# Second expert stage of a fused block: where the last chunk's routing stands, the order of two steps, and the work of the last two steps

## The reference

```python
logits = xt @ router_w.T
topk_vals, topk_idx = jax.lax.top_k(logits, TOP_K)      # 2 of 8
g = jax.nn.sigmoid(topk_vals)
g = g / (g.sum(axis=-1, keepdims=True) + 1e-10)
for e in range(E):
    ge = jnp.sum(jnp.where(topk_idx == e, g, jnp.zeros_like(g)), axis=-1)
    h = jax.nn.silu(xt @ w_gate[e]) * (xt @ w_up[e])
    out = out + ge[:, None] * (h @ w_down[e])
```

## Time and profile before

| | us |
|---|---|
| median of 3 runs | 830.08 |
| lowest, highest | 828.88, 831.36 |
| the profiled execution | 829.33 |
| its span in the trace | 827.4 |
| PE busy in it | 780.4 (94%) |
| VectorE | 625.3 (76%) |
| ScalarE | 526.0 (64%) |
| POOL | 425.5 (51%) |

### The profile page before, as it was taken

How to read it: one execution, slowest core, us unless ns; L and a number is a source line. 1 busy time by engine, 2 the same in 40 slices (tenths; PEclk the granted TensorE clock), 3 DMA queues, 4 the chain that set the end, 5 groups by cost and what they waited for, 6 DMA issues and landing times.

```text
span 827.4 us, 13529 instructions
## 1 busy us (share of the span) xinstructions
PE 780.4 (94%) x4328; PEld 546.0 (66%) x4328; DVE 625.3 (76%) x1596; ACT 526.0 (64%) x1162; POOL 425.5 (51%) x446
## 2 busy tenths in 40 slices
PE   4989899998799999999999999999999998699996
PEld 2667688886556666666666656666666676588884
DVE  7998678788898766778667597667787677587785
ACT  5566566656667767767757577667667545466653
POOL 1054999974344334424334333343335345499974
PEclk9999999999999999999999999999999999899998
DMA  8012663390000000000000000000011332243201
GB/s 229 1 42 29 136 123 77 66 361 2 2 1 1 1 2 1 1 1 1 1 1 2 1 2 1 1 2 1 10 31 32 39 78 67 52 81 101 65 17 39
DMA packets 51141, 35.16 MB, mean 42 GB/s; under 512 B 2640, under 2 KB 48592, under 8 KB 51072
## 3 DMA queue, kind: packets, MB, share of 16 engines
q1 hardware_dynamic: 51072, 34.30, 16.8%
HBM read 33.04 MB, written 1.25 MB: 41 GB/s over the span
## 4 chain that ended last, share of the span: by engine, by line
PE 66%; DVE 12%; POOL 10%; issue 7%; ACT 4%; DMA 1%; SPq 0%; POOLq 0%; DVEq 0%; ACTq 0%
PE psum L935 14%; PE psum L917 12%; PE psum L902 11%; POOL hid_lo L749 9%; PE psum L249 7%; PE psum L250 5%; PE psum L251 5%; PE psum L520 5%; PE psum L859 4%; DVE prob L1030 2%; ACT x_norm L315 1%; DVE hid L638 1%; DVE hid L618 1%; DVE ln_stats L264 1%; DMA ssm_par<-in_ssm_par 1%
## 5 line engine op out<-in xcount | busy, mean ns | idle before, releaser
L1291 POOL TENSOR_SCALAR prob<-prob,ones 128x512 f32<-128x512 f32 x256 | 175.0, 697 | 271.1 <-DVE ones L1019 271.1
L1198 ACT ACTIVATE prob<-prob,ones 128x512 f32<-128x512 f32 x256 | 183.6, 719 | 124.4 <-DVE ones L1030 124.4
L749 POOL TENSOR_TENSOR hid_lo<-hid,hid_hi 128x512 fp32r<-128x512 f32 x128 | 192.2, 1518 | 82.3 <-ACT hid_hi L567 81.3
L1030 DVE CUSTOM_DVE_ANT_0 prob<-psum,bias_band 128x512 f32<-128x512 f32 x256 | 161.6, 687 | 71.4 <-PE psum L902 70.9
L618 DVE TENSOR_TENSOR hid<-silu,psum 128x512 f32<-128x512 f32 x128 | 87.1, 684 | 54.0 <-PE psum L251 43.6
L638 DVE TENSOR_TENSOR hid<-hid,gate_all 128x512 f32<-128x512 f32 x118 | 115.1, 977 | 14.6 <-DMA gate_all<-gates 1.8
L935 PE MATMUL psum<-probT,v 128*64 128x512 f32 x512 | 124.0, 605 | 0.0
L560 ACT ACTIVATE silu<-psum 128x512 f32<-128x512 f32 x128 | 76.4, 598 | 74.6 <-PE psum L251 73.6
L917 PE MATMUL psum<-ident,prob 128*128 128x128 f32 x1024 | 123.3, 273 | 0.0
L917 PEld LDWEIGHTS psum<-ident,prob 128*128 128x128 f32 x1024 | 114.6, 140 | 10.3 <-issue 2.9
L567 ACT CAST hid_hi<-hid 128x512 fp32r<-128x512 f32 x128 | 78.5, 618 | 48.7 <-DVE hid L638 45.2
(11 more groups left out here) (154 smaller groups left out, 1205.9 us busy)
## 6 DMA issues: line engine op xcount, KB each, us to landing
gate_all<-gates SPq DMA_DIRECT2D x59, 256.0 KB, 5.3
bias_band<-bias_rows SPq DMA_DIRECT2D x16, 448.0 KB, 9.0
w_raw<-in_w_gate SPq DMA_DIRECT2D x16, 128.0 KB, 2.8
w_raw<-in_w_up SPq DMA_DIRECT2D x16, 128.0 KB, 2.8
w_raw<-in_w_down SPq DMA_DIRECT2D x16, 128.0 KB, 3.7
x_res<-in_x SPq DMA_DIRECT2D x4, 256.0 KB, 5.8
out<-x_res SPq DMA_DIRECT2D x4, 256.0 KB, 2.3
wqT<-in_WqT SPq DMA_DIRECT2D x1, 512.0 KB, 7.7
```

The source lines that it names most:

```text
L749: nc.gpsimd.tensor_tensor(m["hid_lo"][:, s % 2, half, :], m["hid"][:, s % DEEP, half, :], m["hid_hi"][:, s % 2, half, :].bitcast(F32), ALU ...
L1030: nc.vector.tensor_tensor_reduce(out=prob[:, buf, h, :], in0=bank[scores_home(n) + h][:, :], in1=row_bias, scale=-1.0, scalar=NEG_START, o ...
L1198: nc.scalar.activation(prob[:, buf, h, :], prob[:, buf, h, :], ACT.Exp, bias=peak[:, buf, h:h + 1], scale=-1.0, accum_out=total[:, buf, h: ...
L1291: nc.gpsimd.tensor_scalar(prob[:, buf, h, :], prob[:, buf, h, :], inv[:, buf, h:h + 1], 1.0, ALU.mult, ALU.mult).then_inc(a_n, 1)
```

## The change

It does two things, both in the second expert stage (k = 1).

**Routing of the last chunk.** On PE, step 6 is opened: `gate_up(6,0)` and `down(4)` now stand ahead of `route_logits`; step 8 is issued in `leave` too, and `route_turn` stands between its `down(6)` and `gate_up(8,1)`, `route_spread` behind that. On VectorE `route_weights` moves ahead of step 7's first product, and `route_pick` ahead of its second. On ScalarE `gates_copy` moves behind step 8's first silu and `high_of(7,1)`. The generic loops begin at step 9 for PE and ScalarE. In `LAST_CHUNK_LATE` the steps 9 and 10 are exchanged: (2,2) is now step 9 and (1,3) step 10.

**The end.** The low parts of (step 30, half 1), (31,0) and (31,1) go from POOL to VectorE (`last_low`, semaphore `hd`). The copy of chunk 2's sums goes ahead of step 31's second silu. `last_down` takes the six matmuls in the order hi·hi, lo·hi, hi·lo for each half and waits for each part only where it is used. The copy, the turn, the add and the output of chunk 3 are done in two halves of 256 columns (`last_sums`, `last_turn`, `last_add`).

The diff:

```diff
--- before.py
+++ after.py
@@ -218,7 +218,7 @@
 
         def moe_sems(k):
             names = ("lg", "lc", "rt", "ex", "ld0", "ld1", "sp", "wu", "wd", "g", "u", "sg", "mul", "gm", "hi", "hl", "d",
-                     "acc", "gt_in", "gt_t", "gt_c", "gd", "gb", "y", "yt")
+                     "acc", "gt_in", "gt_t", "gt_c", "gd", "gb", "y", "yt", "hd", "ya")
             q = {n: sem(f"moe{k}_{n}") for n in names}
             q["bc"] = [[sem(f"moe{k}_bc{par}{c}") for c in range(CH)] for par in range(2)]
             return q
@@ -344,7 +344,7 @@
         LAG = 2
         STEPS_K = CH * E
         BY_CHUNK = [(0, 0), (0, 1), (1, 0), (1, 1), (0, 2), (0, 3), (1, 2), (1, 3)]
-        LAST_CHUNK_LATE = [(0, 0), (0, 1), (1, 0), (1, 1), (0, 2), (1, 2), (2, 0), (2, 1), (0, 3), (1, 3), (2, 2), (2, 3),
+        LAST_CHUNK_LATE = [(0, 0), (0, 1), (1, 0), (1, 1), (0, 2), (1, 2), (2, 0), (2, 1), (0, 3), (2, 2), (1, 3), (2, 3),
                            (3, 0), (3, 1), (3, 2), (3, 3)]
         PAIRWISE = [(0, 0), (1, 0), (0, 1), (1, 1), (0, 2), (1, 2), (0, 3), (1, 3)]
         BY_EXPERT = [(0, 0), (0, 1), (0, 2), (0, 3), (1, 0), (1, 1), (1, 2), (1, 3)]
@@ -510,7 +510,11 @@
 
             q, m, (e, c) = MOE[k], MEM[k], ORDER[k][s]
             w_hi, w_lo = weights_of(k, e)
-            pe.wait_ge(q["hl"], 2 * s + 2)
+            if k == 1 and s == STEPS_K - 2:
+                pe.wait_ge(q["hl"], 2 * s + 1)
+                pe.wait_ge(q["hd"], 1)
+            else:
+                pe.wait_ge(q["hl"], 2 * s + 2)
             if s == FIRST[k][e]:
                 pe.wait_ge(q["wd"], e + 1)
             for h in range(MT):
@@ -537,7 +541,7 @@
 
         def experts_tensor(pe, k, turn_in):
 
-            for s in range(8, END + 4):
+            for s in range(8 + k, END + 4):
                 expert_step(pe, k, s)
             expert_step(pe, k, END + 4)
             sums_turn(pe, k, 0)
@@ -550,6 +554,33 @@
             gate_up(pe, k, END + 7, 1)
             down(pe, k, END + 6)
 
+        def last_down(pe):
+
+            q, m, s = MOE[1], MEM[1], STEPS_K - 1
+            e, c = ORDER[1][s]
+            w_hi, w_lo = weights_of(1, e)
+            assert (e, c) == (E - 1, CH - 1)
+            for h in range(MT):
+                col = slice(2 * FH + h * D, 2 * FH + (h + 1) * D)
+                hh, hl = m["hid_hi"][:, s % 2, h, :], m["hid_lo"][:, s % 2, h, :]
+                for n, (w, r) in enumerate(((w_hi, hh), (w_lo, hh), (w_hi, hl))):
+                    if n == 0:
+                        pe.wait_ge(q["hi"], 2 * s + h + 1)
+                    if n == 2:
+                        pe.wait_ge(q["hd"], h + 2)
+                    last = nc.tensor.matmul(bank[4 + c][:, :], w[:, col], r, start=False,
+                                            stop=(h == MT - 1 and n == 2), skip_group_check=True)
+            last.then_inc(q["d"], 1)
+
+        def last_turn(pe):
+            c = CH - 1
+            for part in range(2):
+                pe.wait_ge(MOE[1]["ya"], part + 1)
+                for n in (2 * part, 2 * part + 1):
+                    last = nc.tensor.transpose(bank[part][:, (n % 2) * P:(n % 2 + 1) * P],
+                                               MEM[1]["y_sum"][:, c, n * P:(n + 1) * P], ident[:, :])
+                last.then_inc(MOE[1]["yt"], 1)
+
 
 
         def silu_of(act, k, s, half):
@@ -604,8 +635,17 @@
             high_of(act, k, END + 6, 1)
             if k == 0:
                 ln_high(act, 2, 0, 4)
+            else:
+                sums(act, k, 2)
             silu_of(act, k, END + 7, 1)
             high_of(act, k, END + 7, 0)
+
+        def last_sums(act):
+            c = CH - 1
+            act.wait_ge(MOE[1]["d"], STEPS_K)
+            for part in range(2):
+                cols_ = slice(2 * P * part, 2 * P * (part + 1))
+                nc.scalar.copy(MEM[1]["y_sum"][:, c, cols_], bank[4 + c][:, cols_]).then_inc(MOE[1]["ya"], 1)
 
 
 
@@ -675,14 +715,41 @@
                 gated(dve, 0, END + 6, 1)
             else:
                 vector_step(dve, k, END + 5)
-                vector_step(dve, k, END + 6)
+                product(dve, 1, END + 6, 0)
+                gated(dve, 1, END + 6, 0)
+                product(dve, 1, END + 6, 1)
+                gated(dve, 1, END + 6, 1)
+                product(dve, 1, END + 7, 0)
+                gated(dve, 1, END + 7, 0)
+                last_low(dve, END + 6, 1)
+                product(dve, 1, END + 7, 1)
+                gated(dve, 1, END + 7, 1)
+                last_low(dve, END + 7, 0)
+                add_sums(dve, 1, 1)
+                last_low(dve, END + 7, 1)
+                add_sums(dve, 1, 2)
+                for part in range(2):
+                    last_add(dve, part)
+                return
             add_sums(dve, k, 1)
             product(dve, k, END + 7, 0)
             gated(dve, k, END + 7, 0)
-            if k == 0:
-                ln_low(dve, 2, 0, 4)
+            ln_low(dve, 2, 0, 4)
             product(dve, k, END + 7, 1)
             gated(dve, k, END + 7, 1)
+
+        def last_low(dve, s, half):
+            q, m = MOE[1], MEM[1]
+            dve.wait_ge(q["hi"], 2 * s + half + 1)
+            dve.wait_ge(q["d"], s - 1)
+            nc.vector.tensor_tensor(m["hid_lo"][:, s % 2, half, :], m["hid"][:, s % DEEP, half, :],
+                                    m["hid_hi"][:, s % 2, half, :].bitcast(F32), ALU.subtract).then_inc(q["hd"], 1)
+
+        def last_add(dve, part):
+            dve.wait_ge(MOE[1]["yt"], CH + part)
+            n = (CH - 1) * QT + 2 * part
+            xc = x[:, n:n + 2, :].rearrange("p n d -> p (n d)")
+            nc.vector.tensor_tensor(xc, bank[part][:, 0:2 * P], xc, ALU.add).then_inc(MOE[1]["acc"], 1)
 
 
 
@@ -1004,10 +1073,15 @@
                 part(4, 1)
                 ln_turn(pe, 3, 3, JOB_BANK)
                 expert_step(pe, 1, 5)
+                gate_up(pe, 1, 6, 0)
+                down(pe, 1, 4)
                 route_logits(pe, 1, 3, JOB_BANK)
-                expert_step(pe, 1, 6)
+                gate_up(pe, 1, 6, 1)
                 expert_step(pe, 1, 7)
+                gate_up(pe, 1, 8, 0)
+                down(pe, 1, 6)
                 route_turn(pe, 1, 1)
+                gate_up(pe, 1, 8, 1)
                 route_spread(pe, 1, 3)
 
             return turn_in, enter, steady, leave
@@ -1176,12 +1250,12 @@
                 product(dve, 1, 6, 1)
                 gated(dve, 1, 6, 1)
                 route_index(dve, 1, 1, 3, 4)
+                route_weights(dve, 1, 1)
                 product(dve, 1, 7, 0)
                 gated(dve, 1, 7, 0)
-                route_weights(dve, 1, 1)
+                route_pick(dve, 1, 1)
                 product(dve, 1, 7, 1)
                 gated(dve, 1, 7, 1)
-                route_pick(dve, 1, 1)
 
             return enter, steady, leave
 
@@ -1279,7 +1353,11 @@
                 route_exp(act, 1, 1)
                 high_of(act, 1, 6, 0)
                 scalar_step(act, 1, 7)
+                silu_of(act, 1, 8, 0)
+                high_of(act, 1, 7, 1)
                 gates_copy(act, 1, 1)
+                silu_of(act, 1, 8, 1)
+                high_of(act, 1, 8, 0)
 
             return enter, steady, leave
 
@@ -1343,10 +1421,14 @@
             sp.wait_ge(a_m, 2 * GATES_AT)
             first_gates(sp, 1, 0)
             experts_sync(sp, 1)
-            for c in range(CH):
+            for c in range(CH - 1):
                 sp.wait_ge(MOE[1]["acc"], c + 1)
                 sp.dma_start(ot[:, c * QT:(c + 1) * QT, :], x[:, c * QT:(c + 1) * QT, :]).then_inc(s_out, 16)
-            sp.wait_ge(s_out, 16 * CH)
+            for part in range(2):
+                two = slice((CH - 1) * QT + 2 * part, (CH - 1) * QT + 2 * part + 2)
+                sp.wait_ge(MOE[1]["acc"], CH + part)
+                sp.dma_start(ot[:, two, :], x[:, two, :]).then_inc(s_out, 16)
+            sp.wait_ge(s_out, 16 * (CH + 1))
 
         @block.tensor
         def _(pe):
@@ -1472,8 +1554,8 @@
             leave()
             experts_tensor(pe, 1, lambda: None)
             sums_turn(pe, 1, 2)
-            down(pe, 1, STEPS_K - 1)
-            sums_turn(pe, 1, 3)
+            last_down(pe)
+            last_turn(pe)
 
         @block.scalar
         def _(act):
@@ -1571,8 +1653,7 @@
             leave()
             experts_scalar(act, 1)
             high_of(act, 1, STEPS_K - 1, 1)
-            for c in (2, 3):
-                sums(act, 1, c)
+            last_sums(act)
 
         @block.gpsimd
         def _(pool):
@@ -1733,8 +1814,6 @@
             steady()
             leave()
             experts_vector(dve, 1)
-            for c in (2, 3):
-                add_sums(dve, 1, c)
 
 
 # ---- launch: one core; inputs and outputs as the reference has them ----
```

## The result

| | before | changed |
|---|---|---|
| median, us | 829.50 (4 runs beside the changed kernel's) | 817.13 (4 runs) |
| lowest, highest | 828.88, 831.36 | 816.15, 818.59 |
| ratio, 95% interval | | 0.9853, 0.984 to 0.9865 |
| the profiled execution, its span | 829.33, 827.4 | 818.59, 816.6 |

12.4 us faster; the forecast was 816.6.

A forecast was written before the change was run, and what follows sets the result against it. PE and POOL were taken as full in the second expert stage, leaving only places where PE stands still. Routing 9.8 plus end 3.65 gave 13.45 us gained: 830.1 - 13.5 = 816.6 us, 8-in-10 range 814.6 to 820.5.

The forecast's parts named there:

- The routing stretch: Second expert stage, 692 to 718 us: step 9 was to start at 708.5 instead of 718.32, 9.8 us gained.
- Rival A: PE's clock falls in the new idle ahead of `gate_up(8,0)`: gain 11.9 to 10.6, time 818.2 to 819.5 us; chance 0.25.
- A: Distance on PE from the start of step 5's last matmul to step 9's first: before 26.68, forecast 16.86 us.
- C: Distance from `down(30)`'s first matmul to the end of the last add: before 8.95, forecast 5.3 us.
- Rivals B: PE loses nearly all waits ahead of step 9, which starts at 707.8 or earlier: gain 14.2 to 15.5 us; chance 0.13.
- E: Gates still the last arrival at the turn, 6 us waiting kept; only the end's 3.65 gained, 826.4 us; chance 0.01.
- The gates by DMA: Step 10, pair (1,3): its gates, coming through DRAM, cost 0; at a landing of 15.7 us, 8.4.
- B: Distance on PE from step 9's first matmul to `down(30)`'s first: before 97.41, forecast 97.4 us.
- Rival C: Gate load takes over 7.3 us, or the end brings under 1.5: gain 8 to 10.5, 819.5 to 822 us; chance 0.09.
- Rival D: Steps 9 to 23: POOL falls behind, PE waits every step; at 1.04 us each 15.6 lost, 832.2 us; chance 0.02.
- The end: From 813 us, last low parts, last `down` and halved output: 3.65 us gained, between 2.5 and 4.1.
- D: Distance from the end of the last add to the span's end: before 2.72, forecast 2.7 us.

The follow-up runs named there:

- the kernel with the silu first: Changed kernel with (2,3)'s gates loaded early, plus ScalarE's first silu of step 7 directly behind the exponential: span 814.7 us, one execution, against 814.8 without it.
- The early load: Changed kernel with SP issuing the gate load of (2,3) directly behind that of (1,3): median 816.23 us, ratio 0.9835.

## Why the prediction was right

**The routing stretch, right in sum and in its places.** Forecast 9.8 gained, measured 9.93. The idle ahead of `gate_up(6,0)` was to be 0.5 and is 0.48; ahead of `gate_up(8,0)` 1.1, and is 1.29, released by VectorE's `product` as said; turn and spread have none. With the 1.8 by which this execution was late beforehand taken off, step 9 starts at 708.4, forecast 708.5. Small errors cancelled. The work without stalls is within 0.3 of the 14.1 that I had, but each break in the row of matmuls costs more than its bracket: from 703.79 to 705.48 is 1.69, which is 1.46 above the pitch, with 1.29 shown, and 693.45 to 694.33 is 0.65 above it with 0.48 shown. Against this, the router, the turn and the spread took 1.2 us (697.54 to 698.34, 708.34 to 708.36, 709.84 to 710.20) where 1.55 stood in the sum. VectorE's held instruction was the cast, the first of the seven, and not the fifth as before: 0.9 longer than alone, where the fifth was 1.1.

**Rival A, the clock, did not come.** The granted clock is 1.00 from 692 to 710. Nine of the ten later kernels have the changed routing, and in the one trace of each the clock is 1.00 from 690 to 712 as well. What I had not made a term of its own is how much of the gain is the clock: about 3.0 of A's 9.93, and 0.96 of C's 3.58. The forecast has both only because it set absolute times at full clock against times read from the trace.

**Rivals B and E did not come.** B wanted the small instructions to slip in before POOL. They do so in the kernel with the silu first, where A is 1.3 longer and not 0.7 shorter; that is no clean test, since its roundings moved too. For E the turn should have waited, and it waits for nothing.

**The gates by DMA: the step that was wrong.** "Cost 0" for (1,3) held, since it waits for nothing in step 10. I had written that SP's later loads stand behind it as before and had not costed them. The fourth of them is (2,3)'s. Step 9 now starts 0.5 us behind the issue of the store, where it was 6.0 us, so step 11 asks 5.5 us sooner after it; and the load, now issued right behind the burst, lands after 10.9 us, not after the middle 5.3. In B this cost 1.0 us, by way of POOL: `gated` late by 1.66, `high_of` late, POOL's rows late, then PE by 0.98 at 729.27. The early load shows it as the cause. Rival C had the right queue but the wrong load, and weights, which it named as a reason, were not being loaded.

**Steps 9 to 28.** Rival D did not come: behind the one stall B is as before to 0.2. Its price can now be told from a run: POOL has 0.5 us in hand per step, so a backlog of the size seen here is worked off and does not stay. "POOL and PE are both full", read from the earlier trace rows, was too strong for POOL.

**The end, right in size.** `down(30)` to the last add: 5.37, forecast 5.3. The halves were to bring 0.85 in C. They bring 0.39 there; the other 0.46 is the turns' clock, which ran at 1.2 GHz in the trace that the sum was read from. Behind the last add I had taken 2.7 unchanged, and there the last half brings 0.25: D is 2.40 to 2.49 in eight of the nine traces with halves (2.78 in one), 2.68 to 2.72 in the three without. The `down` part was to bring 2.8 with 0.6 clock; it brought 2.23 without the clock and 0.49 with it, 2.7. That `down(30)` would start "as before" held: what gained nothing was saved from a loss of 0.44.

**The sum.** 12.6 by the distances against 13.45 forecast: 0.13 better in A, 1.16 worse in B, 0.07 worse in C, 0.26 better in D. The medians' 12.4 is within 0.2 us of it. The forecast of the time, 816.6, is off by 0.5 only, less than the gain's 1.1, by luck: it was laid on a median before of 830.1, which is 829.5 over the four runs here.

## What to carry to other kernels

When a change pulls a stretch of work forward, look at every transfer whose start did not move with it, not only at the first: here the fourth load of a burst was the late one, and moving its issue ahead of two others gave back 1.0 of the 1.16 us lost. A queue that reads 100% busy may have slack in rows that stretch, and an idle ahead of one instruction may be the best place for it; the distance between two fixed instructions of the bottleneck engine, which takes in both, is what to compare, above all where the part ahead scatters by more than the change brings.

## What the runs showed of the hardware

- A small instruction on VectorE that starts while POOL runs one can last until POOL's is over. The cast of 128x8, 0.16 us alone, took 1.08 and ended with POOL's row (703.36 against 703.32); two picks of 128x32, 0.28 together, took 2.50 while POOL ran three lows back to back.
- It goes both ways: POOL's 128x512 subtraction took 1.29 us where it started first and 1.81 where VectorE's `gated` started 0.04 ahead of it. The row of a held instruction counts as busy.
- A stop in a row of matmuls costs about 0.17 us more than the idle that is shown (0.65 for 0.48, 1.46 for 1.29), a gap of 0.24 showed no idle at all, and the first matmul behind a stop takes 0.31 to 0.35 to the next start instead of 0.23.
- The granted clock fell to 1.2 GHz at the end of one execution and not of another with the same instructions and idles (1.44 and 0.56 against 1.43 and 0.55). An idle is not enough to tell, from one trace of each, whether it will.
- Of four loads of 256 KB that one queue issued within 2 us, with no other load under way, the first landed after 4.6 us and the last after 10.9, twice the middle of 5.3.
